# Two gaps of 64 bytes in the layout of on-chip memory: the attention weights and the MLP's square weights begin at another offset

## What is computed

```python
x = layernorm(x + gated_conv_mixer(x))      # projection to 2*256, grouped causal convolution of 4 taps, SiLU gate, small MLP
x = layernorm(x + mixture_of_experts(x))    # 8 experts, top 2, SwiGLU with 352 hidden features
x = layernorm(x + feature_attention(x))     # 16 heads of 8, 32 exponential features for each, no softmax matrix
x = layernorm(x + ternary_mlp(x))           # see below

def ternary_mlp(x, w1, s1, w2, s2, h1, t1, h2, t2, w3, s3):     # w1, w2: 512x128, h1, h2: 512x512, w3: 128x512
    h = silu(x @ w1.T * s1) * (x @ w2.T * s2)
    h = gelu(h @ h1.T * t1)
    h = gelu(h @ h2.T * t2)
    return h @ w3.T * s3
```

## The kernel before

| buffer | before | mod 128 | mod 512 | after | mod 128 | mod 512 |
|---|---|---|---|---|---|---|
| front_hi (first layer's weights) | 82848 | 32 | 416 | 82848 | 32 | 416 |
| w13_hi (moving in the MLP and experts) | 94688 | 96 | 480 | 94688 | 96 | 480 |
| w13_lo | 117216 | 96 | 480 | 117216 | 96 | 480 |
| qk_hi | 139744 | 96 | 480 | 139808 | 32 | 32 |
| om_hi | 141792 | 96 | 480 | 141856 | 32 | 32 |
| fh_hi | 145888 | 96 | 480 | 145952 | 32 | 32 |
| ff_out_w | 178656 | 96 | 480 | 178784 | 96 | 96 |
| xT_hi | 180704 | 96 | 480 | 180832 | 96 | 96 |
| work | 184928 | 96 | 96 | 185056 | 96 | 224 |
| stage | 203168 | 32 | 416 | 203296 | 32 | 32 |
| rT_hi | 225696 | 32 | 416 | 225824 | 32 | 32 |

## Time and profile before

### The profile page before, as it was taken

How to read it: one execution, slowest core, us unless ns; L and a number is a source line. 1 busy time by engine, 2 the same in 40 slices (tenths; PEclk the granted TensorE clock), 3 DMA queues, 4 the chain that set the end, 5 groups by cost and what they waited for, 6 DMA issues and landing times.

```text
span 371.1 us, 8518 instructions
## 1 busy us (share of the span) xinstructions
PE 329.2 (89%) x2540; PEld 300.7 (81%) x2540; DVE 262.4 (71%) x857; ACT 210.3 (57%) x430; POOL 173.3 (47%) x234
## 2 busy tenths in 40 slices
PE   3799999976757999998987999999998999999990
PEld 1698989866647999998976888887787999999990
DVE  3768988868843578678864699986895777666841
ACT  2455777534512455455448688777566766767330
POOL 0023777745572447965588676554111433134200
PEclk9999999998996999999988999999999999999996
DMA  8990011121322625122403000000000000000001
GB/s 266 430 371 0 29 32 31 31 65 43 72 74 65 200 59 172 53 64 71 134 21 119 17 2 2 1 3 0 3 2 1 2 16 15 14 14 1 14 16 32
DMA packets 17033, 23.71 MB, mean 64 GB/s; under 512 B 3424, under 2 KB 14176, under 8 KB 16208
## 3 DMA queue, kind: packets, MB, share of 16 engines
q1 hardware_dynamic: 13712, 17.97, 14.9%
q0 software_dynamic: 2272, 4.69, 3.8%
q10 hardware_dynamic: 1008, 0.53, 0.6%
HBM read 17.45 MB, written 6.73 MB: 65 GB/s over the span
## 4 chain that ended last, share of the span: by engine, by line
PE 60%; DVE 8%; issue 5%; ACT 2%; another core or an unknown queue 2%; POOL 2%; POOLq 0%; DVEq 0%; ACTq 0%
PE ps L1962 9%; PE ps L1963 9%; PE ps L1599 7%; PE ps L1601 6%; PE ps L1600 6%; PE ps L1799 5%; PE ps L1907 4%; PE ps L2025 3%; PE ps L1788 3%; PE ps L1922 3%; ACT sb_stage L735 1%; PE ps L1934 1%; PE ps L1864 1%; DVE sb_stage L1310 1%
## 5 line engine op out<-in xcount | busy, mean ns | idle before, releaser
L1962 PE MATMUL ps<-sb_w_hi,sb_fh_hi 128*128 128x256 f32 x256 | 63.4, 287 | 1.1 <-DVE sb_w_lo L914 0.6
L1963 PE MATMUL ps<-sb_w_lo,sb_fh_hi 128*128 128x256 f32 x256 | 62.2, 283 | 0.0
L1962 PEld LDWEIGHTS ps<-sb_w_hi,sb_fh_hi 128*128 128x128 f32 x256 | 49.0, 191 | 2.2 <-issue 1.0
L1963 PEld LDWEIGHTS ps<-sb_w_lo,sb_fh_hi 128*128 128x128 f32 x256 | 49.0, 191 | 0.0
L459 POOL DMA_INDIRECT routed<-sb_rows_of,sb_row x32 | 32.0, 1000 | 16.5 <-issue 10.2
L1599 PE MATMUL ps<-sb_w_hi,sb_rT_hi 128*128 x78 | 30.2, 387 | 8.8 <-issue 3.5
L1799 PE MATMUL ps<-sb_w,sb_stage 128*128 x234 | 34.5, 285 | 1.5 <-issue 1.1
L607 POOL TENSOR_TENSOR sb_w_lo<-sb_x_in,sb_w_hi 128x256 fp32r<-128x256 f32 x24 | 17.5, 757 | 36.9 <-DVE sb_w_hi L1535 36.9
L1799 PEld LDWEIGHTS ps<-sb_w,sb_stage 128*128 128x128 f32 x234 | 30.7, 200 | 2.3 <-issue 2.0
L558 POOL DMA_INDIRECT answers<-sb_stage x24 | 25.0, 1043 | 12.4 <-issue 6.7
L579 POOL TENSOR_TENSOR sb_w_lo<-sb_x_in,sb_w_hi 128x512 fp32r<-128x512 f32 x16 | 20.7, 1294 | 20.3 <-DVE sb_w_hi L1396 20.2
(11 more groups left out here) (304 smaller groups left out, 1040.8 us busy)
## 6 DMA issues: line engine op xcount, KB each, us to landing
sb_stage<-in_w SPq DMA_DIRECT2D x2, 1408.0 KB, 13.2
sb_stage<-routed SPq DMA_DIRECT2D x24, 65.0 KB
sb_w<-in_w SPq DMA_DIRECT2D x1, 1536.0 KB, 17.7
sb_x_in<-in_x_tok SPq DMA_DIRECT2D x1, 1024.0 KB, 8.8
sb_x_in<-in_ff_h SPq DMA_DIRECT2D x1, 1024.0 KB
sb_xT_in<-in_ff_h SPq DMA_DIRECT2D x1, 1024.0 KB
sb_got_first<-answers SPq DMA_DIRECT2D x4, 256.0 KB, 2.6
sb_w<-answers SPq DMA_DIRECT2D x4, 256.0 KB, 3.6
```

What stands on the lines that cost most here:

```text
L1962: mm(dst, w_hi, x_hi, start=start, stop=False)
L1963: last = mm(dst, w_hi, x_lo, start=False, stop=stop and exact)
```

## The change

A buffer of 64 bytes that nothing reads or writes is put between `w13_lo` and `qk_hi`, and another one between `fh_lo` and `ff_out_w`. The six buffers qk_hi, qk_lo, om_hi, om_lo, fh_hi and fh_lo thus begin 64 bytes later, and everything from `ff_out_w` on 128 bytes later. What lies before `qk_hi` stays. Every engine's instructions are the same as before, in the same order and with the same waits, only with other addresses, so no piece of the order is shown.

```diff
         w13_lo = sb("w13_lo", [P, EXPERTS, 2 * HIDDEN], f32r)
+        sb("gap_before_qk", [P, 16])
         qk_hi, qk_lo = sb("qk_hi", [P, 2, P], f32r), sb("qk_lo", [P, 2, P], f32r)
         om_hi, om_lo = sb("om_hi", [P, 2, 2 * P], f32r), sb("om_lo", [P, 2, 2 * P], f32r)
         fh_hi, fh_lo = sb("fh_hi", [P, 2 * FF_TILES, FF], f32r), sb("fh_lo", [P, 2 * FF_TILES, FF], f32r)
+        sb("gap_after_fh", [P, 16])
         ff_out_w = sb("ff_out_w", [P, FF_TILES, D])
```

## The result

The changed kernel is faster by 0.74%: 363.58 us (median of 20 runs, 360.49 to 367.58) against 366.39 us for the kernel before in as many runs beside it (362.74 to 368.95). The ratio is 0.9926, with a 95% interval of 0.990 to 0.9952. Some runs of either kernel fell in a slower state at a lower clock and are left out of the ratios, which are therefore not exactly those of the medians. The forecast was 360.1 us, 1.0% less than a median of 363.78 us. The direction was right, the size too large, and the mechanism that the forecast named is not the one that the experiments found. A part of the miss is the base: three runs had given 363.78 us where twenty give 366.39.

The account below looks back on a forecast made before the run. The prediction took PE to bound the kernel in the MLP and nearly so in attention. Gains of 3.1 us (MLP) and 0.6 us (attention), 0 elsewhere, made 3.7 us: 363.8 to 360.1 us, 1.0% less, range 358.6 to 365.5 us.

Parts of the forecast that it names:

- What bounds the kernel: PE, never idle in the steady MLP and nearly so in attention, so each ns per product shows in the total.
- If the remainder by 128 of the weights decides: Square products in the MLP: weights moving from 96 to 32 by 128 cut each from 120.0 to 113.3 ns.
- second rival: MLP: distance between weights and moving operand counts, period for example 512 bytes; 1.0 us less, 362.8 us; chance 0.10.
- The experts as evidence: Expert products, weights at 32 by 128, cost 160 ns, 13.3 above their columns; counted as strong support for no effect.
- 3.1 us in the MLP: Square products 6.7 ns shorter: 2.1 us from 320 in the steady part, 0.9 us from about 140 elsewhere.
- 0.6 us in attention: 144 products with om or qk as weights, 6.7 ns less each: 1.0 us, taken as 0.6 us.
- 0 for the rest, 128 bytes later: Buffers xT, work, hT, stage, rT, ff_out_w keep their remainder by 128: 0, with -2 and +2.5 us for the range.
- The slower rival: Experts and convolution: a period above 128 bytes costs 6.7 ns per product, about 2.5 us, 366.3 us; chance 0.11.
- No effect: MLP: the 6.7 ns come from something else, such as PSUM use; time stays 363.8 us; chance 0.27.
- The base: Whole kernel: the gain was subtracted from 363.8 us, the median of three runs of the kernel before.
- 106.7 ns for the columns alone: Lower bound for a 256-column product, from 0.417 ns a column; at most 13.3 ns each, 6.8 us, could go.

## Why the prediction was right or wrong

**What bounds the kernel: right.** PE is without a gap in the steady part of the MLP before and after, and what the products lost the turn lost: 0.36 us in the 56-run, 0.35 us in the turn.

**"If the remainder by 128 of the weights decides": wrong, and this is the step that failed.** The forecast took a correlation in one trace (weights at 32 faster than weights at 96) for the cause. The number that it gave for the turns was right, 113.3 ns forecast and 113.6 measured, but by luck: the first layer, which lent the number, lies 64 bytes behind the moving operand, and the change happened to put the square weights 64 bytes ahead of it. What counts is the distance to the moving operand by 256 bytes: 0 before, 64 after. The forecast named this as its second rival and priced it from the convolution's 118 ns at 1.0 us less. The pair moved by 32 bytes shows that the rival's mechanism was the right one. Its period was too long, 256 instead of 512, and its price too low. That the convolution was a poor neighbour for the price (its distances differ from product to product, and 118 ns is also what the slower mode has) is my reading and not shown.

**The experts as evidence.** I had counted their 160 ns with weights at 32 by 128 against my own forecast, and rightly: it was a sign that an offset alone does nothing. They stay at 160 to 162 ns in every kernel (median from the start of the second or third product of an `mm3` to the next), at distances of 0, 32, 64, 128 and 192 among others, so the interplay is different or hidden in products of 352 columns. Why is open.

**3.1 us in the MLP: too large, and this is the term that was mis-sized.** It was 2.0 us, and 2.4 us in the changed kernel run again (94.68 to 92.32 us). The forecast knew one time for a product at its new place, and there are two. In the steady part 1.76 us came (5 turns of 0.35) where 2.1 was written. A turn gave 0.36 us in the 56-run, but only 0.01 us where 8 square products stand behind the output layer (1.04 to 1.03 us, since they run at 117.8 ns there), and it lost 0.02 us in the first layer's four products, which now take 117 ns each. Outside of the steady part 0.3 us came where 0.9 was written. Half of what is missing is the slower mode: in the execution of the changed kernel that ran its runs of 32 at 114 ns instead of 118 it was 0.6 us. For the rest I had credited all products in runs without a gap, while part of them run at 117.8 ns in both executions, as those of the last batch do, and some runs end in a wait for another engine, which a shorter run only makes longer: the 16 square products that begin at 282.12 us before and at 275.91 us after took 1.92 and 1.83 us, and what lies between them and the next square product grew by as much, from 0.69 to 0.78 us.

**0.6 us in attention: about right by size, by the wrong step.** The forecast misread: it took the row for products with om and qk as weights, but nine of its eleven are key products, with om as the moving operand. Their weights don't move and I had priced them at 0, yet they got shorter, 120 to 117 ns. For them it is the distance that changed.

**0 for the rest, 128 bytes later: right**, 1.002 by its own experiment. The slower rival would have needed a price there, and there is none.

**No effect: out.** The use of PSUM, which this rival had for the 6.7 ns, is the same in all kernels, and the 6.72 us still went to 6.36. By the Trainium skill, "SBUF — State Buffer", "Who interferes with whom", PE never waits on anyone and its two read ports are independent. Read as "the layout can't matter", the runs differ from that: with the same instructions and only the places changed, 56 products take 6.36 or 6.72 us. The measurement decides. That the two reads of PE meet in the memory is my reading of it; the runs show the dependence on their distance, not the place where they meet.

**The base.** 3 runs of before had a median of 363.78 us, 20 runs have 366.39 us. Of the 3.5 us by which 360.1 missed 363.58, 2.6 are this and 0.9 is the size of the gain. The runs of the kernel before are spread over 6 us here, and two of the three shown happened to be low. (The three lie 5.5 us apart, not 5.2 as the prediction has it.)

**106.7 ns for the columns alone** remains an estimate. The prediction's 40 / 96 compares a product at distance 0 (120 ns) with one of the experts (160 ns, distance 192). Against the 113.3 ns of the first layer, which has that distance, the same step gives 0.49 ns for a column and not 0.417.

## What to carry to other kernels

When PE is bound by back to back fp32r products, read the distance between starts, not the mean duration. For products of 128x128 by 256 columns, 120 ns instead of 113.4 was a matter of layout; for those of 352 columns no layout tried changed anything. Keep stationary and moving operands from beginning at the same place by 256 bytes; 64 bytes apart was the best here, though not in every context. A difference within one trace is a hypothesis. To make it a cause, move both operands together and each alone. And look at every run of a product in the trace, not at one kind: here the turns alone suggested a rule for the distance of 192 that the runs ahead of them refute.

## What the runs showed of the hardware

The time of a 128x128 by 256 product in fp32r depends on where the weights begin relative to the moving operand, and a period of 256 bytes fits: 120.0 ns at 0 and 256, 113.4 to 118.7 ns at 32, 64, 96, 128 and 192, all at a granted clock of 1.00 (2.4 GHz). A common shift of 32 bytes of all three operands changes nothing (6.72 and 6.37 us for 56).

At distances of 64 and 192 a chain of products can run in one of two modes with identical addresses, 113.4 or 117.8 ns, and often stays in the one it has for dozens of products. With all weights 64 ahead one turn of five was fast. Two executions of the changed kernel ran the same 32 products in 3.85 and in 3.72 us, so addresses and instructions alone don't pick the mode. What does is open: neither the sign of the distance nor having come out of products at distance 0 did it.

The kernel before took 366.1 and 366.0 us in two sets of runs and 374.0 and 374.8 us in two others, 2% apart and each on another chip. The kernels with distance 0 took the same time within 0.01 us for the 56 products on three of these chips (first, second and third set), and 94.66 to 94.75 us for the whole MLP. In their profiled executions, with spans of 364.7, 371.5 and 374.6 us, the MLP began at 259.5, 266.3 and 269.5 us. So whatever made the difference there lies ahead of the MLP.
